# Six row-max steps moved from six heads into groups 4 to 6, in a kernel of attention and a ternary feed-forward layer

## The chip, the cores and the metric

The kernel runs on one core of a Trainium2 chip. The metric is the device time of one execution in microseconds. The engines are TensorE (PE, with its weight loads as PEld), VectorE (DVE), ScalarE (ACT), GpSimd (POOL) and SyncE (SP), which issues most of the DMAs. Each engine works its own list of instructions in order; semaphores tie the lists together.

## The reference

For x of 2 x 2048 x 256 in float32:

```python
xn = layernorm(x)                                  # no gain, no bias
# attention branch: a second layernorm with gain and bias, then
z = layernorm(xn) * g + b
q, _, v = split(z @ w_in.T + b_in, 3);  k = q      # 16 heads of width 16, keys = queries
p = softmax(q @ k.T / 4)                           # 2048 x 2048 for each of 2 x 16 heads
attn = (p @ v) @ w_out.T + b_out
# feed-forward branch
h = gelu(xn @ ternary(W1).T + b1)                  # 256 -> 1024
ffn = h @ ternary(W2).T + b2                       # 1024 -> 256
out = x + attn + ffn
```

Because keys equal queries the score matrix of a head is symmetric. The kernel works with a maximum for each of the 2048 rows, which it needs before it can take the exponentials of that head.

## The kernel before, in words

**Two stages.** The 4096 tokens are cut into 8 groups of 512. The first stage goes through the groups 0 to 7. For each group it normalises (DVE), transposes (PE, L1159), forms q and v (PE, L1124), stores q to memory, forms the 1024 hidden features in 8 slices f = 0 to 7 (PE, L1187), applies GELU (ACT, L1052), splits the result into two half-precision parts (ACT L1057, DVE L875), and, in the next group's turn, takes the second feed-forward product (PE, L1104). The second stage goes through the 32 heads (2 batches x 16).

**Row-max steps.** The maximum of a head's rows is computed in NA = 32 steps. A step is a pair of PE matmuls of 512 columns into one of two pairs of PSUM banks (`a_step`, L358) and one DVE maximum over the 1024 columns (`max_step`, L883). Step n may be issued on PE only when the maximum of step n-2 is done, because there are two bank pairs (banks 0-1 and 2-3). A step takes the key and query copies of its own head, which stand in three rotating buffers.

**Heads.** A head has 64 score tiles of 128 x 512. PE forms one into a ring of three banks (`b_chunk`, L399, which waits until the exponential three tiles back is done), ACT takes its exponential (L1081), and once four tiles of a block are there PE multiplies them with v, in two halves of four column groups (`pv_half`, L385); block 0 of a head is taken whole, in one piece. The product accumulates in one bank over the 16 blocks of the head, and ACT copies it out (L1068) before block 0 of the next head may write there; this copy stands behind the fifth exponential of the next head (`EVAC_AT = 4`).

**The order on PE** in a head is 8 times the string `BBAPBBAPBBAPBBAP`: B is a score tile, A a row-max step, P a half product. In the first of the eight, the first two P are the last block of the head before, the third does nothing (block 0, first half), and the fourth is block 0 whole. The A steps run ahead of the head that PE works on: the lead is 8 steps (`STEPS * AHEAD`), so in head h come steps 8 to 31 of head h+1 and then steps 0 to 7 of head h+2. No row-max step is left in the last quarter of head 30 and in head 31.

**The first steps.** The row-max steps of head 0 and the first 8 of head 1 are put into the first stage. Groups 2 to 6 take four each: on PE behind slices f = 0, 1, 3 and 5 (`BETWEEN`), on DVE as two, one and one ahead of the first three L875 instructions of the group (`ROWS_AT`). Group 7 takes six between the down products of group 6 (`EARLY`), six behind its own slices (`BETWEEN_LAST`) and eight between its own down products. The transposes of a group write the banks 0, 1 and 2, which the row-max steps use too. So they wait on PE for all the maxima of the groups before:

```python
wait(pe, s_r, step_count(g))     # L1156, ahead of the transposes L1159 of group g
```

**Around them.** POOL forms the split of a head's maxima when all 32 are there (`split_max`), and SP transposes them and writes them into two rows of the head's query buffer (`max_rows_in`); the first score tile of the head waits for that. SP loads the copies of head h+2 when PE has formed the last score tile of head h-1.

Of the kernel before, what the change touches and what calls it, by code (L numbers as in the profile page):

```python
# [20 lines left out]
ROT = 3  # L21
# [9 lines left out]
XS = 256.0  # L31
HTOP = 2.0 ** 14

AHEAD = 2
STEPS = 4
WARM = 16
PERIOD = "BBAPBBAPBBAPBBAP"


def wait(eng, sem, value):  # L40
# [5 lines left out]
def attention_ffn(nc, x, cols, rows, w_qv, w_o, w_1, w_2, ident, out):  # L46
    NB, L, C = x.shape
# [3 lines left out]
    NH = NB * H  # L51
# [5 lines left out]
    NT = NB * L // P  # L57
    NG = NT // TG
    HC = P // D
    NPER = NBLK // 2  # L60
    NA = NBLK * (NCH // 2)
    NE = NBLK * NCH
    W = 2 * BANK
# [12 lines left out]
    with ctx:  # L76
# [242 lines left out]

        BETWEEN = (0, 1, 3, 5)
        BETWEEN_LAST = (1, 2, 3, 4, 5, 6)
        ROWS_AT = (2, 1, 1, 0)
        ROWS_AT_LAST = (2, 2, 2, 0)
        EARLY = 6
        HALF_GROUPS = NG // NB // 2
        HALF_STEPS = NBLK // 2
        assert HALF_STEPS + len(BETWEEN) * (NG - 1 - NG // NB) + EARLY + len(BETWEEN_LAST) == NA
        assert HALF_STEPS == len(BETWEEN) * HALF_GROUPS  # L330
        FILL = 2

        def row_step(h, a):
# [16 lines left out]
        def a_step(eng, h, v, a):  # L350

            pair = pa[a % 2]
            wait(eng, s_r, NA * h + a - 1)
            blk, side = row_step(h, a)
            for j in range(2):
                c = 2 * side + j
                r = tile(c)
                mm = eng.matmul(pair[:, j * BANK:(j + 1) * BANK], key[v][r:r + ROWS, blk * P:(blk + 1) * P],  # L358
                                qry[v][r:r + ROWS, c * BANK:(c + 1) * BANK], start=True, stop=True)
            mm.then_inc(s_a, 1)  # L360
# [41 lines left out]
        def pe_head(eng, j, k, fill=None):  # L402

            h = j * ROT + k
            first = h == 0
            left = NH - 1 - h
            i, kb, x = 0, -1, 0
            for q in range(NPER):

                steps = iter([(1 if q + AHEAD < NPER else 2, STEPS * ((q + AHEAD) % NPER) + n) for n in range(STEPS)])  # L410
                for what in PERIOD:
                    if what == "B":
                        b_chunk(eng, h, k % ROT, i // NCH, i % NCH)
                        i += 1
                    elif what == "P":
                        if first and kb + x <= 0:
                            for _ in range(FILL):
                                fill()
                        elif kb >= 0:
                            if first and kb == 0:  # L420
                                eng.wait_ge(s_ra, 2 * NG)
                            pv_half(eng, h, kb, x)
                        elif not first:
                            pv_half(eng, h - 1, NBLK - 1, x)
                        kb, x = kb + x, 1 - x
                    else:
                        ahead, a = next(steps)
                        if left >= ahead:
                            if a == 0:
                                eng.wait_ge(s_ld[(k + ahead) % ROT], 128 * (j + (k + ahead) // ROT + 1))  # L430
                            a_step(eng, h + ahead, (k + ahead) % ROT, a)

# [287 lines left out]
        def _(dve):  # L722
# [142 lines left out]
            def results(g, rows=None):  # L865
                for i in range(KF // 2):
                    if rows:
                        rows((ROWS_AT_LAST if g == NG - 1 else ROWS_AT)[i])
                    if i == KF // 2 - 1:
                        value(g, 0)  # L870
                    dve.wait_ge(s_h1, KF // 2 * g + i + 1)
                    if g == 0 and i == 0:
                        dve.wait_ge(s_wd, 8)
                    part = [p[:, 2 * i:2 * i + 2, :] for p in parts_of(g)]
                    dve.scalar_tensor_tensor(out=part[1], in0=hid[:, 2 * i:2 * i + 2, :], scalar=hs[:, 0:1], in1=part[0],  # L875
                                             op0=ALU.mult, op1=ALU.subtract).then_inc(s_h2, 1)
# [22 lines left out]
            out_scale()  # L899
            results(0)  # L900

            steps = iter([(0, a) for a in range(NA)] + [(1, a) for a in range(STEPS * AHEAD)])

            def first_rows(n):
                for _ in range(n):
                    max_step(*next(steps))
# [19 lines left out]
            q_split(g)  # L926
            results(g, first_rows)
            value(g, 1)
            first_rows(STEPS * AHEAD - 1)
            add_ffn(g, 1)  # L930
            first_rows(1)

# [2 lines left out]
                dve.reciprocal(rsum[n], sums[n]).then_inc(s_rc, 1)  # L935

            for h in range(1, NH):
                for a in range(STEPS * AHEAD if h == 1 else 0, NA):
                    max_step(h, a)
                    if h == 1 and a == STEPS * AHEAD + 1:  # L940
                        add_ffn(NG - 1, 0)
                if h in (H + 3, H + HC + 3):
                    recip(0 if h < H + HC else 1)
# [41 lines left out]
        def _(act):  # L985
# [89 lines left out]
            def head(h, k, first=False, last=False):  # L1075
                for i in range(NE):
                    kb, c = i // NCH, i % NCH
                    act.wait_ge(s_b, NE * h + i + 1)
                    if c == 0 and not (first and kb < 2):
                        act.wait_ge(s_pv, NBLK * h + kb - 1)  # L1080
                    act.activation(prob[kb % 2][:, c * BANK:(c + 1) * BANK], ring_bank(k, i, last), ACT.Exp,  # L1081
                                   scale=exp_scale).then_inc(s_e, 1)
                    if i == EVAC_AT and not first:
                        evacuate(h - 1)
                    if last and c == NCH - 1 and kb % TG == 0 and kb:
                        evacuate_last(kb // TG - 1)
# [8 lines left out]
        def _(pe):  # L1095
# [47 lines left out]
                    mm = pe.transpose(tr_f[:, t * P:(t + 1) * P], f_rep[:, t, :], idf[:, :])  # L1143
                mm.then_inc(s_ft, 1)

            def step_count(g):

                return len(BETWEEN) * (min(max(0, g - HALF_GROUPS), HALF_GROUPS) + max(0, g - NG // NB))

            def group(g, between=None, between_down=None):  # L1150
                pe.wait_ge(s_ln, 4 * g + 4)
                wait(pe, s_x2, KC * g)
                if g == 1:
                    pe.wait_ge(s_wd, 5)
                    pe.wait_ge(s_od, 1)
                wait(pe, s_r, step_count(g))  # L1156
                for k in range(KC):
                    for t in range(TG):
                        mm = pe.transpose(tr_x[k][:, t * P:(t + 1) * P], xn[:, t, k * P:(k + 1) * P], idf[:, :])  # L1159
                mm.then_inc(s_tr, 1)  # L1160
                first = g == 0
                if first:
                    abs_total(0)
                factor_transposes(g)
                if first:
                    pe.wait_ge(s_wqp, 1)
                    pe.wait_ge(s_sg, 9)
                else:
                    values(g - 1, 1)
                    ffn_down(g - 1, between_down)  # L1170
                wait(pe, s_vd, 2 * g)
                pe.wait_ge(s_x2, KC * (g + 1))
                pe.wait_ge(s_fr, g + 1)
                for o in range(KC):
                    mm = part_products(pq[o], lambda k, i, n: wqp[:, i, k, o * P:(o + 1) * P],
                                       lambda k, i, n: xp[n][:, k, :], BANK)
                    mm.then_inc(s_q, 1)
                if first:
                    pe.wait_ge(s_wd, 4)
                for f in range(KF):  # L1180
                    if f < 2:
                        wait(pe, s_ra, 2 * (g - 1) + f + 1)
                    else:
                        pe.wait_ge(s_g, KF * g + f - 1)
                    for k in range(KC):
                        for i, part in enumerate(xp):
                            mm = pe.matmul(pf[f % 2], w1t[:, k, f * P:(f + 1) * P], part[:, k, :],  # L1187
                                           start=(k == 0 and i == 0), stop=(k == KC - 1 and i == 1))
                    mm.then_inc(s_h, 1)
                    if first and f == 1:  # L1190
                        abs_total(1)
                        pe.wait_ge(s_oa, 1)
                        for k in range(KC):
                            mm = pe.matmul(bound_o, ones[:, :], abso[:, k, :], start=(k == 0), stop=(k == KC - 1))
                        mm.then_inc(s_ob, 1)
                    if f == 3:
                        values(g, 0)
                    if between and f in (BETWEEN_LAST if g == NG - 1 else BETWEEN):
                        between()


            pe.wait_ge(s_c, 1)
# [10 lines left out]
            pe.matmul(sum_b1, ones[:, :], b1abs[:, KF:KF + 1], start=True, stop=True).then_inc(s_qb, 1)  # L1213
            pe.wait_ge(s_id, 16)
            group(0)
            steps = iter([(0, a) for a in range(NA)] + [(1, a) for a in range(STEPS * AHEAD)])

            def first_a():
                h, a = next(steps, (None, None))
# [68 lines left out]
```

## Time and profile before

| | |
|---|---|
| three runs, median | 1402.43 us (1400.91 to 1403.2) |
| the profiled execution, its own time | 1403.4 us |
| its span | 1401.6 us |
| mean granted TensorE clock | 0.994 |
| PE busy | 1368.6 us (98%), 13350 matmuls |
| DVE busy | 1328.5 us (95%), 1396 instructions |
| ACT busy | 1238.4 us (88%), 2244 instructions |
| POOL busy | 141.5 us (10%) |
| chain that ended last | DVE 70%, PE 23%, DMA 3%, issue 2%, ACT 1% |
| of it DVE row maxima, L883 | 67% |

Busy times are unions of instructions, whose recorded durations overlap the next one's a little. The pitch, from start to start, is what an instruction costs its engine. Matmuls overlap more: four of them on different parts of the array run side by side, and their ends are modelled. A busy PE is therefore not a PE at its limit.

### The profile page before, as it was taken

What the parts mean: (1) busy time and instruction counts of PE and PEld (TensorE: products, weight loads), DVE (VectorE), ACT (ScalarE), POOL (GpSimd) and SP (SyncE); (2) the same over time, 40 slices, a digit from 0 to 9 for tenths busy, and PEclk for the clock granted to TensorE, in tenths of its full rate; (3) what the DMA queues carried; (4) which work ended last, traced back from release to release, by engine and by line L of the source; (5) the groups of instructions that cost most, each with busy time, mean ns of one, the idle gap of its engine ahead of it and who ended that gap; (6) DMA issues with size and microseconds to landing.
All of it is one profiled execution on the core that took longest, in us unless ns stands there. A gap on an engine that the chain in (4) does not pass through costs nothing.

```text
span 1401.6 us, 32162 instructions
## 1 busy us (share of the span) xinstructions
PE 1368.6 (98%) x13350; PEld 468.3 (33%) x13350; DVE 1328.5 (95%) x1396; ACT 1238.4 (88%) x2244; POOL 141.5 (10%) x351
## 2 busy tenths in 40 slices
PE   6999999999999999999999999999999999999999
PEld 4656643222222222222222222222222222222244
DVE  6898999999999999999999999999999999999934
ACT  5564638999999999999999999999999999999965
POOL 2101034000000000000000000000222200002200
PEclk8999999999999999999999999999999999999999
DMA  6012000000010000001000101011121100012122
GB/s 238 27 39 64 31 18 2 32 33 33 33 33 33 32 33 33 33 33 33 33 33 32 33 32 35 29 35 37 57 65 57 50 32 33 32 35 62 40 106 81
DMA packets 33916, 61.75 MB, mean 44 GB/s; under 512 B 11392, under 2 KB 16928, under 8 KB 33514
## 3 DMA queue, kind: packets, MB, share of 16 engines
q1 hardware_dynamic: 33194, 58.04, 12.3%
q8 instruction: 105, 1.72, 0.5%
q10 hardware_dynamic: 576, 1.65, 0.3%
q14 instruction: 41, 0.34, 0.1%
HBM read 41.29 MB, written 16.77 MB: 41 GB/s over the span
## 4 chain that ended last, share of the span: by engine, by line
DVE 70%; PE 23%; DMA 3%; issue 2%; ACT 1%; POOL 0%; SPq 0%; ACTq 0%; DVEq 0%; POOLq 0%
DVE part_max L883 67%; PE ps L385 6%; PE ps L1187 3%; PE ps L399 3%; PE ps L1104 3%; PE ps L358 3%; PE ps L1124 2%; PE ps L476 1%; DMA rows<-in_rows 1%; PE ps L457 1%; ACT w L1081 1%; DMA max_rows<-max_split 1%; DMA w_ternary<-o_recip 0%; PE ps L446 0%; PE ps L486 0%
## 5 line engine op out<-in xcount | busy, mean ns | idle before, releaser
L1081 ACT ACTIVATE w<-ps 128x512 f32<-128x512 f32 x2048 | 1111.2, 595 | 68.8 <-PE ps L446 19.5
L883 DVE TENSOR_REDUCE part_max<-ps 128x1 f32<-128x1024 f32 x1024 | 1161.1, 1212 | 3.9 <-PE ps L358 3.6
L385 PE MATMUL ps<-w,v_ones 128*32 128x256 f32 (+1 forms) x7688 | 627.1, 398 | 0.7 <-DVE resid L804 0.3
L399 PE MATMUL ps<-qry,key 50*128 50x512 f16 x1984 | 398.6, 386 | 8.0 <-ACT w L1081 6.9
L358 PE MATMUL ps<-qry,key 48*128 48x512 f16 x2048 | 393.9, 380 | 4.9 <-DVE part_max L883 4.7
L385 PEld LDWEIGHTS ps<-w,v_ones 128*32 128x32 f32 x7688 | 151.4, 108 | 313.2 <-issue 160.1
L399 PEld LDWEIGHTS ps<-qry,key 50*128 50x128 f16 x1984 | 98.1, 92 | 430.2 <-ACT w L1081 411.4
L358 PEld LDWEIGHTS ps<-qry,key 48*128 48x128 f16 x2048 | 100.0, 93 | 81.8 <-DVE part_max L883 15.7
L675 POOL COPY v_ones<-v_all 128x128 f32<-128x128 f32 x64 | 18.7, 293 | 749.1 <-PE ps L385 749.1
L1048 ACT ACTIVATE q_split<-q_by_factor,sigma_bq 128x512 f16<-128x512 f32 x16 | 11.1, 719 | 63.3 <-DVE q_by_factor L785 62.9
L1187 PE MATMUL ps<-x,w_ternary 128*128 128x512 f16 x256 | 62.1, 381 | 1.6 <-ACT hidden L1052 1.6
L1104 PE MATMUL ps<-w_ternary,w 128*128 128x256 f16 x448 | 51.3, 273 | 0.5 <-DVE w L875 0.5
L1052 ACT ACTIVATE hidden<-ps,columns 128x512 f32<-128x512 f32 x64 | 41.7, 678 | 6.5 <-PE ps L1187 5.5
L1104 PEld LDWEIGHTS ps<-w_ternary,w 128*128 128x128 f16 x448 | 43.3, 98 | 7.0 <-issue 1.4
L875 DVE SCALAR_TENSOR_TENSOR w<-hidden,hidden_scale,w 128x1024 f16<-128x1024 f32 x28 | 35.7, 1281 | 6.5 <-ACT w L1057 6.5
L949 DVE SCALAR_TENSOR_TENSOR resid<-ps,y_unscale,resid 128x512 f32<-128x512 f32 x16 | 11.8, 744 | 30.1 <-PE ps L476 29.9
L682 POOL TENSOR_TENSOR max_rise<-part_max 128x16 f32<-128x16 f32 x32 | 7.9, 247 | 274.2 <-DVE part_max L883 274.2
L1187 PEld LDWEIGHTS ps<-x,w_ternary 128*128 128x128 f16 x256 | 22.5, 98 | 32.6 <-issue 6.5
L1057 ACT ACTIVATE w<-hidden,hidden_scale 128x1024 f16<-128x1024 f32 x28 | 32.2, 1149 | 1.0
L1124 PE MATMUL ps<-x,wq_parts 128*128 128x512 f16 x96 | 24.6, 410 | 3.7 <-ACT factor_rows L1020 3.7
L651 POOL TENSOR_TENSOR rstd<-var_eps,minus_half 128x8 f32<-128x8 f32 x8 | 13.5, 1690 | 118.5 <-DVE var_eps L758 118.5
L1124 PE MATMUL ps<-wv_parts,x 128*128 128x256 f16 x192 | 23.6, 273 | 0.0
(151 smaller groups left out, 486.9 us busy)
## 6 DMA issues: line engine op xcount, KB each, us to landing
key<-q_parts SPq DMA_DIRECT2D x62, 128.0 KB
qry<-q_parts SPq DMA_DIRECT2D x62, 128.0 KB
o_heads<-o_evacuated SPq DMA_DIRECT2D x31, 256.0 KB, 9.7
key<-q_parts SPq DMA_DIRECT2D x66, 64.0 KB
qry<-q_parts SPq DMA_DIRECT2D x66, 64.0 KB
resid<-in_x SPq DMA_DIRECT2D x8, 512.0 KB, 13.9
q_parts<-q_split SPq DMA_DIRECT2D x16, 256.0 KB, 2.3
out<-resid SPq DMA_DIRECT2D x7, 512.0 KB, 2.9
```

Source lines behind the costliest of these rows:

```text
L358: mm = eng.matmul(pair[:, j * BANK:(j + 1) * BANK], key[v][r:r + ROWS, blk * P:(blk + 1) * P], qry[v][r:r + ROWS, c * BANK:(c + 1) * BANK] ...
L385: mm = eng.matmul(pv[32 * c:32 * c + 2 * D, c0:c1], vst[:, kb, :], prob[kb % 2][:, c * BANK + c0:c * BANK + c1], start=(kb == 0), stop=(kb ...
L399: eng.matmul(ring_bank(v, i, False), key[v][r:r + KROWS, kb * P:(kb + 1) * P], qry[v][r:r + KROWS, c * BANK:(c + 1) * BANK], start=True, s ...
L675: pool.tensor_copy(vst[:, k0:k0 + NBLK // 2, 0:D], v_all[:, ds(b * NBLK + k0, NBLK // 2), ds(hh * D, D)]).then_inc(s_vs, 1)
L875: dve.scalar_tensor_tensor(out=part[1], in0=hid[:, 2 * i:2 * i + 2, :], scalar=hs[:, 0:1], in1=part[0], op0=ALU.mult, op1=ALU.subtract).th ...
L883: dve.tensor_reduce(part_max[h % 2][:, blk, side:side + 1], pa[a % 2], AX.X, ALU.max).then_inc(s_r, 1)
L1052: act.activation(hid[:, f, :], pf[f % 2], ACT.Gelu, scale=1.0 / XS, bias=b1_col[:, f:f + 1]).then_inc(s_g, 1)
L1057: act.activation(parts_of(g)[0][:, f - 1:f + 1, :], hid[:, f - 1:f + 1, :], ACT.Identity, scale=hs[:, 0:1]).then_inc(s_h1, 1)
L1081: act.activation(prob[kb % 2][:, c * BANK:(c + 1) * BANK], ring_bank(k, i, last), ACT.Exp, scale=exp_scale).then_inc(s_e, 1)
L1104: mm = pe.matmul(pf[t // 2][:, (t % 2) * C:(t % 2 + 1) * C], parts_of(g)[i][:, f, t * P:(t + 1) * P], w2t[:, f, :], start=(f == 0 and i == ...
L1124: mm = pe.matmul(out, rows(k, i, j), cols(k, i, j), start=(m == 0), stop=(m == len(terms) - 1))
L1187: mm = pe.matmul(pf[f % 2], w1t[:, k, f * P:(f + 1) * P], part[:, k, :], start=(k == 0 and i == 0), stop=(k == KC - 1 and i == 1))
```

## The change

Groups 4, 5 and 6 take six row-max steps each in place of four: on PE one behind slices f = 0 and 1 and two behind f = 3 and 5; on DVE two ahead of each of the first three L875. The six added steps carry the row-max steps further: group 7's own six behind its slices are now steps 0 to 5 of head 1, and the lead at the start of head 0 is 14 steps. Six heads (4, 8, 12, 16, 20, 24) then have 31 steps in place of 32, so that the lead is 8 again from head 25 on. In these heads the first of the eight strings is `BBAPBBAPBBAPBPB`: it has no fourth A, and the eighth score tile stands behind the whole product of block 0. Also in these heads ACT copies the output of the head before behind the fourth exponential in place of the fifth. The wait ahead of a group's transposes counts the steps as they now lie.

```diff
-AHEAD = 2
-STEPS = 4
+QUARTERS = 8
+SPARE = 6
+LAST_STEPS = 8
 PERIOD = "BBAPBBAPBBAPBBAP"
+PERIOD_SKIP = "BBAPBBAPBBAPBPB"
...
-        BETWEEN = (0, 1, 3, 5)
-        BETWEEN_LAST = (1, 2, 3, 4, 5, 6)
-        ROWS_AT = (2, 1, 1, 0)
-        ROWS_AT_LAST = (2, 2, 2, 0)
+        BETWEEN_HALF = (1, 1, 0, 1, 0, 1, 0, 0)
+        BETWEEN_FULL = (1, 1, 0, 2, 0, 2, 0, 0)
+        BETWEEN_LAST = (0, 1, 1, 1, 1, 1, 1, 0)
+        ROWS_HALF = (2, 1, 1, 0)
+        ROWS_FULL = (2, 2, 2, 0)
+        ROWS_LAST = (2, 2, 2, 0)
...
+        def step_count(g):
+            return sum(sum(between(n)) for n in range(g))
+
+        LEAD = SPARE + LAST_STEPS
+        SKIPS = [NH // (SPARE + 1) * (n + 1) for n in range(SPARE)]
...
+        def head_steps(h):
+            done = NA + LEAD + NA * h - sum(n < h for n in SKIPS)
+            count = NA - (h in SKIPS)
+            return [divmod(n, NA) for n in range(done, done + count)]
...
+            steps = iter(head_steps(h))
             for q in range(NPER):
-                steps = iter([(1 if q + AHEAD < NPER else 2, STEPS * ((q + AHEAD) % NPER) + n) for n in range(STEPS)])
-                for what in PERIOD:
+                for what in PERIOD_SKIP if h in SKIPS and q == 0 else PERIOD:
...
-            first_rows(STEPS * AHEAD - 1)
+            first_rows(LAST_STEPS - 1)
...
-                for a in range(STEPS * AHEAD if h == 1 else 0, NA):
+                for a in range(LEAD if h == 1 else 0, NA):
...
-                    if i == EVAC_AT and not first:
+                    if i == (EVAC_AT - 1 if h in SKIPS else EVAC_AT) and not first:
                         evacuate(h - 1)
...
-                    if between and f in (BETWEEN_LAST if g == NG - 1 else BETWEEN):
-                        between()
+                    for _ in range(between(g)[f]):
+                        step()
```

## Rows read from the trace of the kernel before

**Rows 1.** Groups of instructions, 450 to 1290 us: shape, count, busy us, mean ns, idle before.
```profile
L883 DVE TENSOR_REDUCE part_max<-ps 128x1 f32<-128x1024 f32 x741 | 838.5, 1210 | 0.1
L1081 ACT ACTIVATE w<-ps 128x512 f32<-128x512 f32 x1481 | 803.8, 595 | 27.9 <-PE ps L399 3.4
```

**Rows 2.** The chain that ended last, in order of time: start us, us, what.
```profile
104.60 0.87 PE ps L1159 x8
...
170.98 0.87 PE ps L1159 x8
...
313.74 35.75 DVE part_max L883 x32
...
856.73 35.75 DVE part_max L883 x32
```

**Rows 3.** Timeline, PE, group 6: start us, us, instruction, count, idle before.
```profile
148.69 1.04 PE L1159 MATMUL ps<-ident_f,xn 128*128 128x128 f32 x8
...
161.85 0.39 PE L358 MATMUL ps<-qry,key 48*128 48x512 f16 x2
162.17 1.04 PE L1187 MATMUL ps<-x,w_ternary 128*128 128x512 f16 x4
...
166.61 0.39 PE L358 MATMUL ps<-qry,key 48*128 48x512 f16 x2
...
168.76 0.39 PE L358 MATMUL ps<-qry,key 48*128 48x512 f16 x2
```

**Rows 4.** Timeline, DVE, group 6.
```profile
161.09 0.69 DVE L785 TENSOR_TENSOR q_by_factor<-ps,factor_rows 128x512 f32<-128x512 f32 x1 [0.23 <-PE ps L1124]
...
163.24 2.35 DVE L883 TENSOR_REDUCE part_max<-ps 128x1 f32<-128x1024 f32 x2
165.51 1.28 DVE L875 SCALAR_TENSOR_TENSOR w<-hidden,hidden_scale,w 128x1024 f16<-128x1024 f32 x1
167.04 1.23 DVE L883 TENSOR_REDUCE part_max<-ps 128x1 f32<-128x1024 f32 x1 [0.25 <-PE ps L358]
...
169.37 1.22 DVE L883 TENSOR_REDUCE part_max<-ps 128x1 f32<-128x1024 f32 x1
```

**Rows 5.** Timeline, PE, at the start of a head.
```profile
1086.13 0.39 PE L358 MATMUL ps<-qry,key 48*128 48x512 f16 x2
1086.36 0.38 PE L399 MATMUL ps<-qry,key 50*128 50x512 f16 x1
1086.96 0.39 PE L399 MATMUL ps<-qry,key 50*128 50x512 f16 x1 [0.23 <-ACT w L1081]
...
1087.58 1.06 PE L385 MATMUL ps<-w,v_ones 128*32 128x512 f32 x8
1088.58 0.39 PE L399 MATMUL ps<-qry,key 50*128 50x512 f16 x2
1088.81 0.38 PE L358 MATMUL ps<-qry,key 48*128 48x512 f16 x2
...
1089.69 0.39 PE L399 MATMUL ps<-qry,key 50*128 50x512 f16 x2
```

**Rows 6.** Timeline, ACT, the same head start.
```profile
1085.68 1.23 ACT L1081 ACTIVATE w<-ps 128x512 f32<-128x512 f32 x2
1086.81 0.59 ACT L1068 ACTIVATE o_evacuated<-ps 128x512 f32<-128x512 f32 x1
1087.28 1.58 ACT L1081 ACTIVATE w<-ps 128x512 f32<-128x512 f32 x3
```

**Rows 7.** Timeline, DVE, the same head start.
```profile
1083.73 3.47 DVE L883 TENSOR_REDUCE part_max<-ps 128x1 f32<-128x1024 f32 x3
```

**Rows 8.** Timeline, PE: two of its longest waits in the groups.
```profile
53.59 1.90 PE L1187 MATMUL ps<-x,w_ternary 128*128 128x512 f16 x8 [1.38 <-ACT hidden L1052]
...
203.90 0.39 PE L358 MATMUL ps<-qry,key 48*128 48x512 f16 x2 [2.19 <-DVE part_max L883]
```

**Rows 9.** Busy time by stretch: length, PE, PEld, DVE, ACT, POOL, clock, DMA, GB/s.
```profile
205.50:209.00 3.50, 3.50 (x16) 1.49 (x14) 2.96 (x3) 0.00 (x0) 3.50 (x6) 0.51 0.03 7
```

More of the change, by code:

```diff
@@ L59, in attention_ffn @@
     HC = P // D
-    NPER = NBLK // 2
+    NPER = QUARTERS
     NA = NBLK * (NCH // 2)
@@ L328, in attention_ffn, with between, rows_at, first_steps @@
         HALF_STEPS = NBLK // 2
-        assert HALF_STEPS + len(BETWEEN) * (NG - 1 - NG // NB) + EARLY + len(BETWEEN_LAST) == NA
-        assert HALF_STEPS == len(BETWEEN) * HALF_GROUPS
+        def between(g):
+            if g < HALF_GROUPS:
+                return (0,) * KF
+            return BETWEEN_HALF if g < NG // NB else BETWEEN_FULL if g < NG - 1 else BETWEEN_LAST
+        def rows_at(g):
+            return ROWS_HALF if g < NG // NB else ROWS_FULL if g < NG - 1 else ROWS_LAST
+        def step_count(g):
+            return sum(sum(between(n)) for n in range(g))
+        LEAD = SPARE + LAST_STEPS
+        SKIPS = [NH // (SPARE + 1) * (n + 1) for n in range(SPARE)]
+        assert step_count(NG) + EARLY == NA + SPARE
+        assert step_count(NG // NB) == HALF_STEPS
+        def first_steps():
+            return iter([(0, a) for a in range(NA)] + [(1, a) for a in range(LEAD)])
+        def head_steps(h):
+            done = NA + LEAD + NA * h - sum(n < h for n in SKIPS)
+            count = NA - (h in SKIPS)
+            return [divmod(n, NA) for n in range(done, done + count)]
         FILL = 2
@@ L405, in pe_head @@
             first = h == 0
-            left = NH - 1 - h
             i, kb, x = 0, -1, 0
+            steps = iter(head_steps(h))
             for q in range(NPER):
-                steps = iter([(1 if q + AHEAD < NPER else 2, STEPS * ((q + AHEAD) % NPER) + n) for n in range(STEPS)])
-                for what in PERIOD:
+                for what in PERIOD_SKIP if h in SKIPS and q == 0 else PERIOD:
                     if what == "B":
@@ L426, in pe_head @@
                     else:
-                        ahead, a = next(steps)
-                        if left >= ahead:
+                        n, a = next(steps)
+                        if n < NH:
                             if a == 0:
-                                eng.wait_ge(s_ld[(k + ahead) % ROT], 128 * (j + (k + ahead) // ROT + 1))
-                            a_step(eng, h + ahead, (k + ahead) % ROT, a)
+                                eng.wait_ge(s_ld[n % ROT], 128 * (n // ROT + 1))
+                            a_step(eng, n, n % ROT, a)
         def last_at(n):
@@ L867, in results @@
                     if rows:
-                        rows((ROWS_AT_LAST if g == NG - 1 else ROWS_AT)[i])
+                        rows(rows_at(g)[i])
                     if i == KF // 2 - 1:
@@ L900, in _ @@
             results(0)
-            steps = iter([(0, a) for a in range(NA)] + [(1, a) for a in range(STEPS * AHEAD)])
+            steps = first_steps()
             def first_rows(n):
@@ L937, in _ @@
             for h in range(1, NH):
-                for a in range(STEPS * AHEAD if h == 1 else 0, NA):
+                for a in range(LEAD if h == 1 else 0, NA):
                     max_step(h, a)
-                    if h == 1 and a == STEPS * AHEAD + 1:
+                    if h == 1 and a == LEAD + 1:
                         add_ffn(NG - 1, 0)
@@ L1144, in factor_transposes, with group @@
                 mm.then_inc(s_ft, 1)
-            def step_count(g):
-                return len(BETWEEN) * (min(max(0, g - HALF_GROUPS), HALF_GROUPS) + max(0, g - NG // NB))
-            def group(g, between=None, between_down=None):
+            def group(g, step=None, between_down=None):
                 pe.wait_ge(s_ln, 4 * g + 4)
@@ L1215, in _ @@
             group(0)
-            steps = iter([(0, a) for a in range(NA)] + [(1, a) for a in range(STEPS * AHEAD)])
+            steps = first_steps()
             def first_a():
```

## The prediction, made before the changed kernel was run

> **What bounds the kernel now.** I read the chain that ended last, then the groups of instructions over the middle heads, then single instructions in one group and at one head start. The chain gives two different regimes. In the groups it runs over PE: the transposes of groups 4 and 7 start at 104.60 and 170.98 [rows 2], three periods apart, so a group takes 66.38 / 3 = 22.13 us. In the heads it runs over DVE: from 313.74 to 856.73 lie 15 heads [rows 2], 542.99 / 15 = 36.20 us each, or 36.20 / 32 = 1.131 us for a row-max step. Over 840 us of heads DVE does 741 maxima, is busy 838.5 us and idles 0.1; ACT idles 27.9 in the same stretch [rows 1]. So in the heads a step taken off DVE is worth up to 1.13 us, if PE and ACT can feed DVE faster. In the groups the question is what two more steps do.
>
> **Part 1: two more steps in each of groups 4, 5 and 6.** I measure from T, the start of the group's transposes on PE, 148.69 for group 6 [rows 3]. The next group's come 22.13 later, at 170.82.
>
> On PE a step costs 162.17 - 161.85 = 0.32 us of issue [rows 3]; two are 0.64. If PE alone set the period, it would become 22.77.
>
> On DVE the order matters, because the next transposes wait for all of the group's maxima. A maximum costs (165.51 - 163.24) / 2 = 1.13 [rows 4]. An L875 costs what remains of 169.37 - 167.04 = 2.33 when one maximum is taken off: 1.19 [rows 4].
> - The maxima start at 163.24, T + 14.55. What stands before them waits for PE's q product (0.23 us at 161.09 [rows 4]), so this distance from T stays.
> - Two maxima, an L875: T + 14.55 + 2.27 + 1.28 = T + 18.10. The third maximum starts as before at 167.04 = T + 18.35, since it waits 0.25 for the matmuls of the step at 166.61 [rows 3, 4].
> - Third and fourth: to T + 20.62. The fourth step's matmuls are put straight behind the third's, 0.32 later, long before that.
> - L875: to T + 21.81. Fifth and sixth: the fifth's matmuls come at 168.76 + 0.32 = T + 20.39 [rows 3], in time; the sixth's need the fourth maximum, done at T + 20.7, also in time. The sixth starts at T + 22.95 and, at a duration of 1.22 [rows 4], ends at T + 24.17.
> - The transposes of the next group follow at about T + 24.2.
>
> Before, the last of four maxima started at 169.37 and ended at 170.59, T + 21.90, 0.23 ahead of the transposes, so PE did not feel it. With two more, PE waits for DVE: the period becomes 24.2, 2.05 us more, of which PE stands still for 24.2 - 22.77 = 1.4. What DVE has left of the group (two L875 and a v pair) starts 0.1 us ahead of the new transposes; before, 0.3 ahead of them. The difference is small and stands beside the transposes and q products of the next group, so nothing is given back and nothing more is lost. For three groups: 3 x 2.05 = +6.2 us. Six steps of DVE are 6.8, so the groups hide almost nothing of them. Bounds: +1.9 (3 x 0.64, PE alone sets the period) and +6.8 (each step pays in full); I take 6.2, because the wait named stands in the code and its last releaser is computed from rows.
>
> Group 7 keeps its number and places of steps; only their head changes, which costs nothing: the copies of head 1 are loaded right after those of head 0, ahead of group 4's q.
>
> **Part 2: six heads with 31 steps.** The saving is 1.131 us a head less what DVE idles at the missing step. At the head start [rows 5 to 7] the DVE maxima start 1.131 apart from 1083.73: at 1086.00, 1087.13, 1088.26. The third A of the head (1086.13) is the one consumed at 1087.13. DVE wants the next at 1088.26. Before, the fourth A was there in time. Now the next A is that of the second string, behind these:
> - the seventh score tile at 1086.36, as before;
> - the output copy. The fourth exponential starts at 1085.68, the copy one pitch of 0.49 later (three in 1.58, of which one lasts 0.60 [rows 6]), at 1086.17, and ends at 1086.76. Block 0's product waits for it: 1086.85, with 0.1 for the hand-over (score tile 1086.96 comes 0.05 behind the exponential that ended at 1086.91 [rows 5, 6]);
> - that product takes 1088.58 - 1087.58 = 1.00 [rows 5]; the eighth tile comes at 1087.85, the ninth beside it. The tenth waits for the seventh exponential: copy 1086.17, then at 0.47, 0.49 and 0.49 the fifth, sixth and seventh, the last from 1087.62 to 1088.22. So tile ten stands at 1088.27, and A another 0.23 on (1088.58 to 1088.81 [rows 5]), at 1088.50;
> - its result is there 0.43 later (166.61 to 167.04 [rows 3, 4]), at 1088.93. DVE has idled 0.67.
>
> The next P waits for the eighth exponential: tile 1087.85, 0.42 to its exponential, 0.60 for it, so about 1088.95; a half product is 0.57 (the period of 1.11 from 1088.58 to 1089.69 less 0.23 for the tiles and 0.31 for A [rows 5]); then tiles and A at 1089.75, data at 1090.18, where DVE wanted it at 1090.06: 0.12 more. From there PE's period of 1.11 is shorter than DVE's 1.131 and DVE runs full again, with PE's lead won back over the head. So a short head saves 1.13 - 0.67 - 0.12 = 0.34 us; six of them 2.0 us. Bounds: 6.8 (DVE never idles) and -0.6 (PE comes another 0.45 late each time, the length of a copy's pitch). I take 2.0.
>
> **Part 3: what costs nothing.** The lead of 14 makes the steps of head h+2 start after 18 steps in place of 24 in the early heads, 18 x 1.13 = 20 us after the load is issued. A head's maxima are complete up to 6 steps earlier, so the split, its DMAs and the queue of SP behind them come earlier, not later. POOL has nothing before them. If a load did come late, each microsecond would be paid once.
>
> **The sum.** 6.2 - 2.0 = +4.2 us. The profiled execution took 1403.4, its span 1401.6; the new one would be 1407.6. The median of the runs is 1.0 below the profiled time, so against it 1406.5.
>
> **Clock.** In the trace a wait of PE of 2.19 us at 203.90 is followed by a stretch at a granted clock of 0.51, the lower level of 1.2 GHz, from 205.5 to 209 [rows 8, 9]; after a wait of 1.38 us at 53.59 [rows 8] the next eight matmuls take 1.90 us, which is the pitch of full clock ((1.90 - 1.04) / 4 = 0.215, against the four in 1.04 of [rows 3]). The new waits of 1.4 us are nearest to the second, so the sum has no term for it. The Trainium skill (TensorE: Matmul & The Clock Gate, The HAM clock gate) says that the throttled state is the default and activity releases it, which would let each new wait end in half clock; the trace bears this out once in the groups, after the longer wait.
>
> **Rivals.**
> - A, DVE is not starved at the short heads (PE prepares the next A in time, or the copy comes earlier than I think). For it: ACT idles 27.9 us in 23 heads [rows 1], 1.2 per head, more than the saving needs. Against: the idle time isn't at the head start, where exponentials already follow at 0.49. It gives 6.2 - 6.8 = -0.6: 1401.8.
> - B, the wait of the transposes is not the binding one, and groups cost only PE's 0.64 or a little more. Against: the arithmetic above, with 0.23 us of slack for 2.27 of work. It gives 1.9 - 2.0: 1402.4; with A, -4.9: 1397.5, the faster side.
> - C, the waits of 1.4 us drop the clock. Half clock for 3.5 us [rows 9] costs 1.75 on work that is all on the path from T to the q product; three times, 5.3: 1411.8. It decides once PE idles as long as at 203.90, 2.19.
> - D, the short heads save nothing or lose 0.1: 1408.5 to 1409.1.
>
> **Chances.** Forecast with its own range of 1405.2 to 1407.8: 0.55. A 0.13, half-way cases between A and the forecast 0.10, B alone or with A 0.08, C 0.05, D 0.09. What a measurement of this kernel can tell from no change is 0.2%, 2.8 us, so slower means above 1405.2 and faster below 1399.6. Forecast, C and D lie above, less what noise and a head saving of 0.6 take off: 0.65. Faster needs B with A, or A with a smaller group cost: 0.07. The rest, 0.28, is within. Range 1401.8 (A's time) to 1409.8 (D with 0.7 of noise), leaving out B with A and C.
>
> **What would show it.** In the trace after: transposes of groups 5, 6 and 7 each with a wait of about 1.4 us on the row maxima and 24.2 us apart (22.13 up to group 4). Heads 4, 8, ... 24 of 35.86 us among others of 36.20, with two short idles of DVE, 0.7 and 0.1, at their start, for PE's L358; the rest of DVE gapless. Wrong if the group period is 22.8 (part 1), if short heads take 35.1 (part 2), or if the clock reads 0.5 behind the new waits (C).

## The result and the profile after

| | before | after |
|---|---|---|
| median of five runs each, same chip | 1401.18 us | 1408.86 us (1407.18 to 1410.56) |
| ratio, with its 95% interval | | 1.0047 (1.0036 to 1.0057) |
| profiled execution, span | 1401.6 us | 1406.4 us |

The change makes the kernel slower, by 7.7 us in the medians and by 4.8 us between the two profiled executions. Over 29 runs the kernel before has a median of 1402.2, which makes it 6.7; the changed kernel has the five runs above.

First the groups. The transposes of groups 4 to 7 on PE (start us, us, instruction, count, idle before and its releaser), which answer to 148.69 in [rows 3]; L1183 is L1159 of before:

```profile
104.25 1.04 PE L1183 MATMUL ps<-ident_f,xn 128*128 128x128 f32 x8
...
128.56 1.06 PE L1183 MATMUL ps<-ident_f,xn 128*128 128x128 f32 x8 [1.32 <-DVE part_max L911]
...
152.89 0.96 PE L1183 MATMUL ps<-ident_f,xn 128*128 128x128 f32 x7 [1.32 <-DVE part_max L911]
...
177.23 1.06 PE ps L1183 x8
```

(The last is the chain's line of the same instructions.) They now lie 24.31, 24.33 and 24.34 apart, where it was 22.13, and each stands 1.32 us for the row maxima. DVE's rows of group 6, which answer to [rows 4], show which one:

```profile
165.32 0.69 DVE L813 TENSOR_TENSOR q_by_factor<-ps,factor_rows 128x512 f32<-128x512 f32 x1 [0.23 <-PE ps L1152]
...
167.47 2.35 DVE L911 TENSOR_REDUCE part_max<-ps 128x1 f32<-128x1024 f32 x2
169.73 1.28 DVE L903 SCALAR_TENSOR_TENSOR w<-hidden,hidden_scale,w 128x1024 f16<-128x1024 f32 x1
171.27 2.36 DVE L911 TENSOR_REDUCE part_max<-ps 128x1 f32<-128x1024 f32 x2 [0.26 <-PE ps L387]
173.54 1.28 DVE L903 SCALAR_TENSOR_TENSOR w<-hidden,hidden_scale,w 128x1024 f16<-128x1024 f32 x1
174.73 2.35 DVE L911 TENSOR_REDUCE part_max<-ps 128x1 f32<-128x1024 f32 x2
177.00 1.28 DVE L903 SCALAR_TENSOR_TENSOR w<-hidden,hidden_scale,w 128x1024 f16<-128x1024 f32 x1
```

The sixth maximum ends at 174.73 + 2.35 = 177.08, and the transposes start at 177.23.

Then a short head. PE, DVE and ACT at the start of head 4, which answer to [rows 5 to 7]:

```profile
369.10 0.39 PE L387 MATMUL ps<-qry,key 48*128 48x512 f16 x2
369.32 0.38 PE L428 MATMUL ps<-qry,key 50*128 50x512 f16 x1
369.87 1.06 PE L414 MATMUL ps<-w,v_ones 128*32 128x512 f32 x8 [0.17 <-ACT o_evacuated L1096]
370.87 0.77 PE L428 MATMUL ps<-qry,key 50*128 50x512 f16 x3
371.25 0.60 PE L387 MATMUL ps<-qry,key 48*128 48x512 f16 x2
```

```profile
366.69 4.61 DVE L911 TENSOR_REDUCE part_max<-ps 128x1 f32<-128x1024 f32 x4
371.89 2.50 DVE L911 TENSOR_REDUCE part_max<-ps 128x1 f32<-128x1024 f32 x2 [0.59 <-PE ps L387]
```

```profile
369.12 0.61 ACT L1096 ACTIVATE o_evacuated<-ps 128x512 f32<-128x512 f32 x1
```

PE waits for the copy, then comes the whole product, three tiles and the next step. DVE's gap from start to start is 371.89 - 370.09 = 1.80 in place of 1.13 (370.09 is the start of the fourth of the four from 366.69): 0.67 lost. The next maximum starts 1.27 behind 371.89 in place of 1.13, so the two take 2.50 where two take 2.35 [rows 4]: another 0.14.

Last, group 7. DVE's groups of instructions from 196.9 to 212 (count, busy us, mean ns, idle before):

```profile
L911 DVE TENSOR_REDUCE part_max<-ps 128x1 f32<-128x1024 f32 x8 | 9.4, 1209 | 0.0
L903 DVE SCALAR_TENSOR_TENSOR weight_scratch<-hidden,hidden_scale,below_half 128x1024 f16<-128x1024 f32 x4 | 6.2, 1556 | 0.0
L824 DVE SCALAR_TENSOR_TENSOR v_all<-ps,factor_columns,scaled_bv 128x256 f32<-128x256 f32 x4 | 1.7, 470 | 0.0
```

and the same of before, 189 to 204:

```profile
L875 DVE SCALAR_TENSOR_TENSOR weight_scratch<-hidden,hidden_scale,below_half 128x1024 f16<-128x1024 f32 x4 | 5.1, 1277 | 0.0
```

L903 takes 1556 ns where it took 1277; the maxima and L824 are unchanged. L817, just ahead in the same group, is slower too (L789 of before, the second line):

```profile
194.07 2.35 DVE L817 SCALAR_TENSOR_TENSOR q_split<-q_by_factor,sigma_bq,q_split 128x512 f16<-128x512 f32 x2 [0.34 <-ACT q_split L1076]
```

```profile
187.63 1.41 DVE L789 SCALAR_TENSOR_TENSOR q_split<-q_by_factor,sigma_bq,q_split 128x512 f16<-128x512 f32 x2 [0.34 <-ACT q_split L1048]
```

What stands beside them is POOL, adding the output bias to the residual (32 additions; L669 is L697 of after). First after, then before:

```profile
193.32 23.99 POOL L697 TENSOR_TENSOR resid<-resid,bias_row 128x256 f32<-128x256 f32 x28
```

```profile
202.26 21.94 POOL L669 TENSOR_TENSOR resid<-resid,bias_row 128x256 f32<-128x256 f32 x32
```

Of the additions after, one that overlaps an L903 and one that overlaps none:

```profile
199.01 1.71 POOL L697 TENSOR_TENSOR resid<-resid,bias_row 128x256 f32<-128x256 f32 x1
...
201.36 0.72 POOL L697 TENSOR_TENSOR resid<-resid,bias_row 128x256 f32<-128x256 f32 x1
```

The one at 199.01 lasts until 200.72, just behind the L903 that DVE has from 198.60 to 200.13; the one at 201.36 runs beside a maximum. Before, POOL began these additions at 202.26, behind all of group 7's L875. Behind the slower group PE waits 3.75 us where it waited 2.19 [rows 8], and the clock is at its lower level for a while (stretch, length, PE, PEld, DVE, ACT, POOL busy, granted clock, DMA share, GB/s):

```profile
211.89 0.61 PE L387 MATMUL ps<-qry,key 48*128 48x512 f16 x2 [3.75 <-DVE part_max L911]
```

```profile
204.00:211.20 7.20, 4.14 (x35) 2.73 (x32) 7.20 (x9) 3.12 (x3) 7.20 (x9) 1.00 0.02 3
211.20:218.00 6.80, 6.11 (x26) 2.63 (x26) 5.34 (x5) 0.00 (x0) 6.11 (x9) 0.51 0.00 0
```

Where the two profiles part, stage by stage, from starts of the same instructions (T is the start of a group's transposes; head n's output copy is the one that ACT makes in head n, of the output of head n - 1):

| stretch | before | after | difference |
|---|---|---|---|
| start to T of group 4 | 104.44 | 104.25 | -0.2 |
| groups 4 to 6, to T of group 7 | 66.38 | 72.98 | +6.6 |
| T of group 7 to the first maximum behind its last v values | 31.80 | 33.39 | +1.6 |
| from there to block 0's product of head 0 | 13.66 | 14.81 | +1.15 |
| from there to head 1's output copy | 36.24 | 35.74 | -0.5 |
| to head 31's output copy, 30 heads | 1088.88 | 1086.93 | -1.95 |
| to the end | 60.2 | 58.3 | -1.9 |
| span | 1401.6 | 1406.4 | +4.8 |

Up to the last copy the two profiles differ by 6.7, as the medians do. That the two numbers agree is partly chance, since not all lines repeat: in a second profile of the kernel before (e8 below) the -0.5 is absent, the 30 heads take 1090.11 and the stretch from T of group 7 to block 0's product of head 0 takes 44.57 where it is 45.46 here. The last line is taken up behind the experiments.

### The profile page after: what moved, and what is told of

Its sections match the earlier page's. It is cut to its first block, busy times and chain, and to the rows that moved or that the text cites. A ratio compares the mean times of both kernels' runs of the same rounds, so it can differ in the third digit from the quotient of the medians.

```text
span 1406.4 us, 32162 instructions
## 1 busy us (share of the span) xinstructions
PE 1371.2 (97%) x13350; PEld 468.2 (33%) x13350; DVE 1330.6 (95%) x1396; ACT 1238.0 (88%) x2244; POOL 143.8 (10%) x351
## 3 DMA queue, kind: packets, MB, share of 16 engines
q8 instruction: 105, 1.72, 0.5%
## 4 chain that ended last, share of the span: by engine, by line
PE 76%; DVE 18%; ACT 2%; issue 2%; DMA 1%; POOL 0%; ACTq 0%; DVEq 0%; POOLq 0%
PE ps L414 33%; PE ps L428 19%; DVE part_max L911 16%; PE ps L387 13%; PE ps L1132 3%; PE ps L1211 2%; PE ps L1152 2%; ACT w L1109 2%; PE ps L504 2%; PE ps L485 1%; DMA rows<-in_rows 1%; PE ps L474 1%; DVE weight_scratch L903 0%; PE ps L1183 0%; PE ps L514 0%
## 5 line engine op out<-in xcount | busy, mean ns | idle before, releaser
L903 DVE SCALAR_TENSOR_TENSOR w<-hidden,hidden_scale,w 128x1024 f16<-128x1024 f32 x28 | 35.6, 1279 | 5.2 <-ACT w L1085 5.2
L1152 PE MATMUL ps<-x,wq_parts 128*128 128x512 f16 x96 | 24.2, 406 | 3.7 <-ACT factor_rows L1048 3.7
L697 POOL TENSOR_TENSOR resid<-resid,bias_row 128x256 f32<-128x256 f32 x32 | 26.8, 872 | 8.1 <-DVE resid L832 8.1
```

The lines of the kernel that those rows point to most:

```text
L1152: mm = pe.matmul(out, rows(k, i, j), cols(k, i, j), start=(m == 0), stop=(m == len(terms) - 1))
```

## The experiments

Each median is to be held against that of the kernel before in the same runs: 1402.57 for the first four, 1402.18 for the rest; the changed kernel's ratio is 1.0047. Most readings are taken from the profiles, where the period of a group and the length of most heads repeat to 0.02 us. The start, group 7, the tail and one place in the middle of the heads do not. Line numbers shift by one or a few where a line was added.

**POOL's bias additions later (e1_bias_late).**

```diff
             pool.wait_ge(s_row, 17)
+            pool.wait_ge(s_ra, 2 * NG - 1)
             for g in range(NG):
                 add_bias(g)
```

> The changed kernel, but POOL starts to add the output bias (32 additions of 128x256) only when the first half of group 7's feed-forward result is added. Theory: in the changed kernel POOL reaches these additions earlier, since head 0's maxima are complete earlier, and they run beside group 7's L817 and L903 on DVE, whose pitch rises from 1.19 to 1.45 us for L903; that is 1.75 us of the time on the path, and the longer wait of PE behind it (3.75 us in place of 2.19) brings the lower clock for longer, 1.1 us more. Then this run is 1.75 to 2.9 us faster than the changed kernel (1408.9), about 1406.5, L903 in group 7 is back at 1.28 us a piece, and group 7 ends as far behind its transposes as before the change. Rival: the slower DVE work comes from the row maxima or from head 1's loads, not from POOL; then nothing changes within 0.3 us.

Measured 1407.24, ratio 1.0031 (1.0019 to 1.0043). DVE's group of L904 (the former L903) in group 7:

```profile
L904 DVE SCALAR_TENSOR_TENSOR weight_scratch<-hidden,hidden_scale,below_half 128x1024 f16<-128x1024 f32 x4 | 5.1, 1278 | 0.0
```

It is back at 1278 ns, and the two L818 (the former L817) at 1.42 us, so POOL was the cause. From T of group 7 to head 1's copy it took 82.43 in place of 83.94, 1.5 less. The ratios differ by 0.16%, 2.2 us, but their intervals overlap. Half of my expectation on the clock fell: PE's wait was back at 2.19 us, and the low stretch was still 6.8 us long.

**No short heads (e2_no_short_heads).**

```diff
-        SKIPS = [NH // (SPARE + 1) * (n + 1) for n in range(SPARE)]
+        SKIPS = []
```

> The changed kernel with no short head: all heads have 32 steps, the lead of 14 stays to the end, so the six steps are missing in the last periods of head 30. Theory: the short heads save 0.32 us each, six of them 1.9; without them the time is 1.9 longer, less 6 x 0.06 us for six periods of head 30 that lose their row-max step and so fall from 1.13 to 1.07: net 1.5 slower than the changed kernel, about 1410.4, and 9 slower than before. Rival: short heads save what a step costs, 1.13 each: then 6.4 slower, about 1415. Rival: they save nothing: within 0.5 us of the changed kernel.

Measured 1410.2, ratio 1.0056 (1.0042 to 1.0070), 1.3 above the changed kernel where 1.5 was expected. The two medians' intervals overlap; the profiles part more clearly. Head 1's to head 31's copy: 1088.54, 1.6 more than in the changed kernel. Both rivals on the worth of a short head are out.

**The missing step in the middle (e3_short_in_middle).**

```diff
-PERIOD_SKIP = "BBAPBBAPBBAPBPB"
+PERIOD_SKIP = "BBAPBBAPBBAPBBP"
...
-                for what in PERIOD_SKIP if h in SKIPS and q == 0 else PERIOD:
+                for what in PERIOD_SKIP if h in SKIPS and q == 4 else PERIOD:
...
-                    if i == (EVAC_AT - 1 if h in SKIPS else EVAC_AT) and not first:
+                    if i == EVAC_AT and not first:
```

> The changed kernel, but the missing step of the six heads is the last of the fifth of the eight strings (BBAPBBAPBBAPBBP), and the output is copied behind the fifth exponential as in all heads. Theory: what eats the saving is the crowd at the head start (copy, whole product, the tile behind it), but PE's own shortest period of 1.11 against 1.131 leaves little: the missing step costs DVE 0.2 to 0.4 us of idle in the middle, and the next head start, met with less lead, 0.1 to 0.3 more. A short head then saves 0.35 to 0.75 in place of 0.32: 0.2 to 2.6 us faster than the changed kernel. Rival: PE is not near its limit outside the head start: 1.0 to 1.1 saved each, 4 to 4.7 us faster. Rival: place doesn't matter, the same time.

Measured 1406.78, ratio 1.0034 (1.0022 to 1.0046). The copies of a short head and the one behind it lie 35.92 + 36.02 = 71.94 apart, against 72.40 for two full heads and 35.55 + 36.54 = 72.09 in the changed kernel: a saving of 0.46 in place of 0.31. PE and DVE at the gap:

```profile
385.96 0.38 PE L387 MATMUL ps<-qry,key 48*128 48x512 f16 x2
386.27 0.64 PE L414 MATMUL ps<-w,v_ones 128*32 128x256 f32 x8
386.84 0.39 PE L428 MATMUL ps<-qry,key 50*128 50x512 f16 x2
387.16 0.64 PE L414 MATMUL ps<-w,v_ones 128*32 128x256 f32 x8
387.74 0.57 PE L428 MATMUL ps<-qry,key 50*128 50x512 f16 x2
387.96 0.56 PE L387 MATMUL ps<-qry,key 48*128 48x512 f16 x2
```

```profile
386.83 1.23 DVE L911 TENSOR_REDUCE part_max<-ps 128x1 f32<-128x1024 f32 x1
388.56 3.49 DVE L911 TENSOR_REDUCE part_max<-ps 128x1 f32<-128x1024 f32 x3 [0.49 <-PE ps L387]
```

From A to A PE takes 2.00 us with one A missing, where two periods are 2.26: it can't hand DVE the next step 1.13 earlier. So outside the head start, too, PE is close behind DVE, and a missing maximum turns mostly into a wait for PE. That the place doesn't matter is out by the profiles (0.15 a head), not by the medians, whose intervals overlap; a saving of 1.0 a head is out too.

**The copy behind the fifth exponential (e4_copy_behind_fifth).** The last hunk of the diff above, alone.

> The changed kernel with the output copied behind the fifth exponential in the short heads too. Theory: block 0's whole product waits for the copy, so PE stands 0.48 us longer there and DVE idles 0.45 more in each short head, which then saves nothing (-0.1): 2.7 us slower than the changed kernel. Rival: the product is held by something else (the exponentials, the ring of tiles): within 0.5 us of the changed kernel.

Measured 1413.07, ratio 1.0079 (1.0065 to 1.0093).

```profile
367.62 0.38 PE L428 MATMUL ps<-qry,key 50*128 50x512 f16 x1
368.80 1.07 PE L414 MATMUL ps<-w,v_ones 128*32 128x512 f32 x8 [0.81 <-ACT o_evacuated L1096]
```

PE stands 0.81 us for the copy in place of 0.17, and a short head is 0.33 longer than a full one (36.53). The copy's place is worth 0.31 + 0.33 = 0.64 a head, 3.9 in all; I had expected 0.45.

**Five steps in a group (e5_five_steps).**

```diff
-SPARE = 6
+SPARE = 3
...
-        BETWEEN_FULL = (1, 1, 0, 2, 0, 2, 0, 0)
+        BETWEEN_FULL = (1, 1, 0, 2, 0, 1, 0, 0)
-        ROWS_FULL = (2, 2, 2, 0)
+        ROWS_FULL = (2, 2, 1, 0)
```

> The changed kernel with three steps moved in place of six: groups 4 to 6 take five steps (PE: behind slices 0, 1, twice 3, once 5; DVE: two, two, one), the lead is 11, and three heads (8, 16, 24) are short. Theory: the transposes of the next group wait for the last maximum, which had 0.23 us to spare at four steps; each further step costs its full 1.13 us less that slack and 0.1 of hand-over. So a group takes 22.13 + 1.0 = 23.1 us, in place of 24.3 with six, and PE stands 0.7 us. Three groups cost 3.0, group 7 1.5 to 2.6 (POOL and clock, as in the changed kernel), three short heads save 0.9: about 1406.5 where the kernel before has 1402.6. Rival: the longer period comes from a wait that one step doesn't reach, and PE's 0.32 a step is what is paid: a period of 22.5.

Measured 1404.32, ratio 1.0018 (1.0008 to 1.0028). T of groups 4 to 7: 23.18, 23.20 and 23.20 apart, with this wait at group 7:

```profile
173.32 1.06 PE L1183 MATMUL ps<-ident_f,xn 128*128 128x128 f32 x8 [0.67 <-DVE part_max L911]
```

Four, five and six steps give 22.13, 23.2 and 24.33: the first added step costs 1.07, the second 1.13, a whole maximum. PE's 0.32 a step is not what is paid. Against the kernel before the run is 2.1 slower where I had expected 3.9. Part of that miss is group 7: the maxima of head 0 are complete later than in the changed kernel, POOL's additions begin at 199.05, and only the last two L903 are slower (1.72 and 1.64 us). From T of group 7 to block 0's product of head 0 that costs 0.7 (46.19 against 45.46, both with 3.4 us at the lower clock), where I had taken over the changed kernel's 1.5 or more.

**Four of the six ahead of the second L903 (e7_maxima_first).**

```diff
-        ROWS_FULL = (2, 2, 2, 0)
+        ROWS_FULL = (2, 4, 0, 0)
```

> The changed kernel with one tuple altered: DVE takes the group's maxima as two, then four, then none ahead of its L903 instructions (2, 4, 0, 0 in place of 2, 2, 2, 0); PE's order is the same. Theory: the transposes wait for the sixth maximum alone, so with one L903 fewer ahead of it it ends 1.0 to 1.2 us earlier; the work put behind it makes DVE late for the next group by 0.5 to 0.8, of which 0.2 is absorbed. A period of 23.5 to 23.8 in place of 24.33: 1.6 to 2.5 us faster than the changed kernel. Rival: DVE as a whole is the bound of the group, and the order doesn't matter: 24.3 stays. Rival: the late second parts hold up PE's down products: 24.3 or more, with PE waiting there.

Measured 1405.21, ratio 1.0024 (1.0016 to 1.0033). DVE and PE in group 6:

```profile
168.70 4.68 DVE L911 TENSOR_REDUCE part_max<-ps 128x1 f32<-128x1024 f32 x4
...
173.30 1.28 DVE L903 SCALAR_TENSOR_TENSOR w<-hidden,hidden_scale,w 128x1024 f16<-128x1024 f32 x1
```

```profile
173.53 1.06 PE L1183 MATMUL ps<-ident_f,xn 128*128 128x128 f32 x8 [0.20 <-DVE part_max L911]
```

The period falls to 23.25, below the 23.5 to 23.8 that I expected, with the same work on both engines and only one L903 fewer ahead of the last maximum. So it is the wait of the transposes for that maximum that is paid, not DVE's load.

**An early step in DVE's wait for POOL (e6_step_in_wait).** The candidate. The core of its edit against the changed kernel, beside e1's and e3's:

```diff
-SPARE = 6
+SPARE = 3
...
-        BETWEEN_FULL = (1, 1, 0, 2, 0, 2, 0, 0)
+        BETWEEN_FULL = (1, 1, 0, 1, 0, 1, 0, 0)
-        ROWS_FULL = (2, 2, 2, 0)
+        ROWS_FULL = (2, 1, 1, 0)
...
                 value(g - 1, 1)
+                if NG // NB <= g:
+                    first_rows(1)
...
+            def first_a_in_down(g):
+                calls = iter(range(TG * KF // 4))
+                def call():
+                    if next(calls) == 0:
+                        pe.wait_ge(s_x2, KC * (g + 1))
+                        pe.wait_ge(s_fr, g + 1)
+                        first_a()
+                return call
```

> A candidate for the best version: groups 4 to 6 take five steps, four where the kernel before has them and one early, on PE between the down products of the group before and on DVE in the 1.04 us in which it waits for POOL's power (L679); three heads (8, 16, 24) short, the missing step in the fifth string; the output's copy behind the fifth exponential; POOL's bias additions late. Theory: the early maximum stands in an idle stretch and is no longer the last before the transposes, so it costs PE's 0.32 only: a period of 22.45 us. Sum against the kernel before: 3 x 0.32 - 3 x 0.46 - 0.5 for head 1's maximum rows that come in time = -0.9, so 1401.7, within the noise of no change. Rival: DVE's chain up to the q product is already tight, and the early step delays the later ones by its whole 1.13: a period of 23.2, 1404.

Measured 1401.32, ratio 0.9992 (0.9983 to 1.0001). The step fills the wait:

```profile
155.73 0.87 DVE L825 SCALAR_TENSOR_TENSOR v_all<-ps,factor_columns,scaled_bv 128x256 f32<-128x256 f32 x2
156.52 1.21 DVE L912 TENSOR_REDUCE part_max<-ps 128x1 f32<-128x1024 f32 x1
157.65 0.16 DVE L793 TENSOR_TENSOR root_of_var<-var_eps,rstd 128x4 f32<-128x4 f32 x1
```

The period is 22.55, 0.42 more than with four steps (0.32 expected). It is faster than the changed kernel, whose interval begins at 1.0036, and can't be told from the kernel before. What a step saves in a short head, 0.46, and what it costs here, 0.42, are as good as equal.

**The kernel before once more (e8_before_again).** Unaltered, one profiled execution.

> The kernel before once more, unaltered, for its profile. In the first profile the last copy's store took 4.4 us to land (2.4 in all profiles since) and the span behind head 31's copy was 60.2 us, against 58.4. Theory: that is chance of the DMA, so this profile shows 58.4 there, and a span near 1399.7; the groups' period of 22.13 and the heads' 36.20 repeat to 0.02. Rival: the change shortened the tail: then it shows 60.2 again.

Measured 1403.01, span 1401.2. The period of the groups repeats (22.13), and so do most heads (36.20). In the middle they don't: from head 18's output copy to head 19's it is 39.19 in place of 37.80. In all ten profiles PE waits 1.39 us there for a maximum, since DVE has a reciprocal ahead of it (893.91 here); in this one alone the lower clock follows (the same columns as above):

```profile
895.40:899.00 3.60, 3.60 (x26) 0.58 (x24) 3.07 (x3) 2.07 (x5) 0.00 (x0) 0.53 0.02 5
```

Nor does head 1 repeat. PE's wait of 0.47 us for its maximum rows, which the first profile has, is absent. The transfer that carries them and the one that waits for it, in the first profile and then in this one:

```profile
242.64 1.12 SPq L558 DMA_TRANSPOSE max_rows<-max_split  x1
246.80 1.30 SPq L561 DMA_DIRECT2D qry<-max_rows  x2
```

```profile
241.07 1.11 SPq L558 DMA_TRANSPOSE max_rows<-max_split  x1
243.30 1.29 SPq L561 DMA_DIRECT2D qry<-max_rows  x2
```

4.16 us lie between them in the first profile, 2.23 in this one. And the tail does not do what I expected: it is 60.6 us. The last copy's store and the load that waits for it:

```profile
1341.19 0.33 SPq L565 DMA_DIRECT2D o_heads<-o_evacuated  x1
```

```profile
1345.38 0.90 SPq L588 DMA_DIRECT2D wq_wv<-o_heads  x1
```

4.2 us lie between them, where in the changed kernel it is 2.4 (1348.71 to 1351.10). Of the ten profiles, both of the kernel before, e6 and e7 have the long form (4.2 to 4.4, a tail of 59.9 to 60.6), the other six the short one (2.0 to 2.4, a tail of 58.3 to 58.8). e7 differs from the changed kernel only in groups 4 to 6, so the form doesn't go with the lead or the short heads. Whether it goes with anything in the change stays open. That the medians differ by 6.7, as the rest of the two profiles does, speaks against it, but weakly: the changed kernel has five runs, and the rest does not repeat either.

## Why the prediction was right, point by point

**Direction and time.** The forecast was slower, 1406.5 (its own terms give 1406.6); the measured 1408.86 lies in the range. That it does is partly luck: the upper end was made from rival D, short heads that save nothing, which did not happen, and the room was used up by something that the prediction had put at nothing. Forecast were +4.2 us, measured are +6.7 to +7.7. Between the profiles it was +4.2 against +4.8, which is luck too: the tail gave 1.9 that no run ties to the steps, and a late transfer in the profile before gave 0.5.

**Part 1, the groups: right.** A period of 24.2 was predicted from the place of the sixth maximum; it is 24.33, +6.6 for three groups in place of 6.2. The missing 0.1 a group stands behind the wait: the chain gives the transposes 1.06 us in place of 0.87 [rows 2]. PE's wait is 1.32 (predicted 1.4). e5 and e7 show the mechanism from two sides: each step pays its whole maximum beyond about 0.1 of slack, and less is paid if less stands ahead of the last one. Rival B is out.

**Part 2, the short heads: right.** Predicted idle times of DVE 0.67 and 0.12, measured 0.67 and 0.14; a saving of 0.34, measured 0.31, six of them 1.9. A is out by e2. D is out, though e4 shows how near it was: with the copy one exponential later the short heads are longer than full ones.

**Part 3, "POOL has nothing before them": wrong.** This is the step that failed, in a place where I had costed an edit at nothing. The earlier completion of head 0's maxima also releases what stands behind `split_max(0)` in POOL's list, the 28 bias additions, while DVE still has L817 and L903 of group 7 to do. In the profiles that is 1.5 to 1.6 us; e1 takes it away. I had asked what comes late and not what comes too early. At equal lengths of the lower clock, from T of group 7 to block 0's product of head 0, it is 47.07 (e3) against 45.46 (before) with 3.4 us of it, and 48.20 (changed) against 46.68 (e1) with 6.8. So Part 1's sentence that group 7 costs nothing falls with it. The -0.5 of the table is no gain of this kind: in e8, with the lead of 8 steps, the maximum rows of head 1 were there in time as well, and what made PE wait 0.47 us for them in the first profile was a transfer of 4.16 us in place of 2.23. That the larger lead would have hidden such a delay is likely, but no run shows it.

**Clock: right for the groups, incomplete behind them.** The new waits of 1.32 us leave the granted clock at 1.00, in all fifteen cases (three in the changed kernel and in each of e1 to e4), so C did not happen. But the row behind the 1.38 us of [rows 8] was a weak ground for giving them no term: in e8 the clock fell behind a wait of 1.39. The stretch at the lower level in group 7 was there before and could have been given a term in the range: it is 3.4 us long in the first profile of before, absent in the second (granted clock 1.00 from 200 to 220 us) and 6.8 in the profile after. Its price is 0.9 to 1.4 us for each 3.4 us, less than the 1.75 of the prediction: from T of group 7 to block 0's product of head 0 it took 44.57, 45.46 and 46.68 us with 0, 3.4 and 6.8 us of it where POOL stays out of the way (e8, before, e1), 47.07 and 48.20 with 3.4 and 6.8 where it doesn't (e3, changed), and in the middle of the heads e8 paid 1.39.

**The sum again.** -0.2 + 6.6 + 1.6 + 1.15 - 0.5 - 1.95 = 6.7, where the prediction had 6.2 - 2.0 = 4.2. Of the 2.5 that lack, 1.6 are POOL and 1.15 the clock; 0.4 more from the groups stands against -0.2 at the start and the -0.5 of the late transfer. Only POOL's part is shown to come with the change. The 1.15 is the second 3.4 us at the lower clock, and three other profiles with the same long wait of PE had only the first.

## What to carry to other kernels

Idle time of an engine is worth having only where the moved work is not the last thing that somebody waits for: DVE idled 2 us in a group, and two maxima of 1.13 placed ahead of a barrier cost 2.2, while one placed in a wait in the middle cost 0.42. Taking work off the bounding engine pays only down to the next one: here PE stood 0.02 us a period behind, and 1.13 us off DVE brought 0.31 to 0.46. When a step completes earlier, list what its completion releases on every engine, and what runs beside it then.

## What the runs showed of the hardware that was not expected

- GpSimd and VectorE held each other up. With POOL's float32 additions beside it, a `scalar_tensor_tensor` with both tensors in SBUF took 1556 ns in place of 1277, and the addition 1.71 us in place of 0.72. Instructions with one input in PSUM (L824, 470 against 482 ns) and the maxima (1209 against 1222) were not touched. The Trainium skill (SBUF — State Buffer, Who interferes with whom) says that a VectorE instruction with two SBUF inputs contends with a GpSimd instruction that reads SBUF. This case's rows agree: 1556 against 1277 ns on one side, 1.71 against 0.72 us on the other.
- The stretch at the lower clock (0.51, that is 1.2 GHz) in group 7 does not follow from the length of PE's wait alone. Behind a wait of 2.19 us it was 0, 3.4, 6.8 and 6.8 us long in four profiles, behind one of about 3.75 us it was 3.4, 3.4, 3.4, 6.8 and 6.8 in five, behind 3.00 us (e5) 3.4. Nor does a short wait exclude it: the same wait of 1.39 us in the middle of the heads was followed by 3.4 us of it in one profile of ten, e8, the one that had none in group 7.
